# Layer 3's first counts, first batch and last batch rearranged in a four-layer graph kernel

## What is computed

```
x = ln(x + L0(x, adj))   # 8 Euler steps of a graph diffusion
x = ln(x + L1(x, adj))   # two-layer graph network with batch norm
x = ln(x + L2(x, adj))   # attention, 4 heads, masked by adj
x = ln(x + L3(x, adj))   # graph attention:
    Wh = x @ W;  s1 = Wh @ a1;  s2 = Wh @ a2
    e  = leaky_relu(s1[i] + s2[j], 0.2), masked by adj
    h  = softmax(e) @ Wh
```

## Time and profile before

| | us |
|---|---|
| median of 3 executions | 977.42 (976.46 to 977.71) |
| the profiled execution, its own time | 978.22 |
| its span from the first to the last instruction | 976.2 |
| TensorE busy | 902.6 (92%) |
| VectorE busy | 638.6 (65%) |
| ScalarE busy | 508.6 (52%) |
| GpSimd busy | 387.3 (40%) |
| TensorE's granted clock, mean | 0.964 of 2.4 GHz |

### The profile page before, as it was taken

How to read it: one execution, slowest core, us unless ns; L and a number is a source line. 1 busy time by engine, 2 the same in 40 slices (tenths; PEclk the granted TensorE clock), 3 DMA queues, 4 the chain that set the end, 5 groups by cost and what they waited for, 6 DMA issues and landing times. The chain is left out here.

```text
span 976.2 us, 20907 instructions
## 1 busy us (share of the span) xinstructions
PE 902.6 (92%) x6004; PEld 647.9 (66%) x6020; DVE 638.6 (65%) x1936; ACT 508.6 (52%) x918; POOL 387.3 (40%) x439
## 2 busy tenths in 40 slices
PE   6999999999999699975789999999999989999994
PEld 5799999999999688732345445554455533677774
DVE  4754554554554676655557777777777753899995
ACT  4323121121121345664356777777777755888883
POOL 4011121021020130000246777777787855365556
PEclk9999999999999899988579999999999998999998
DMA  8000000000000100000033343333433331010111
GB/s 242 22 12 12 12 22 12 16 16 11 22 0 0 39 5 0 0 1 1 19 80 66 74 91 65 81 81 67 95 65 81 82 69 31 12 29 25 32 32 43
DMA packets 34219, 40.66 MB, mean 42 GB/s; under 512 B 6656, under 2 KB 17536, under 8 KB 34176
## 3 DMA queue, kind: packets, MB, share of 16 engines
q1 hardware_dynamic: 33072, 40.00, 17.2%
q10 hardware_dynamic: 1104, 0.13, 0.1%
HBM read 6.43 MB, written 4.19 MB: 11 GB/s over the span
## 5 line engine op out<-in xcount | busy, mean ns | idle before, releaser
L1681 DVE CUSTOM_DVE_ANT_0 junk<-bank,mask_ij 128x512 bf16<-128x512 f32 x256 | 166.6, 688 | 78.9 <-PE bank L1763 76.9
L1546 POOL TENSOR_TENSOR half_sum<-prob 128x1024 f32<-128x1024 f32 x64 | 151.7, 2379 | 15.6 <-ACT prob L1619 13.6
L1619 ACT ACTIVATE prob<-wide 128x1024 f32<-128x1024 f32 x128 | 125.2, 1017 | 39.4 <-PE wide L1780 35.9
L431 ACT CAST yT<-wide 128x512 fp32r<-128x512 f32 x48 | 28.1, 589 | 206.1 <-PE wide L827 156.7
L531 POOL TENSOR_TENSOR Xr<-Xf,Xr 128x512 fp32r<-128x512 f32 x16 | 20.4, 1291 | 168.1 <-ACT Xr L426 167.9
L1763 PE MATMUL bank<-qkT 32*128 32x512 f32 x256 | 79.6, 516 | 7.9 <-DVE mx L1681 6.9
L1776 PE MATMUL wide<-qk_st 128*128 128x512 f32 x256 | 76.9, 423 | 1.0 <-issue 0.7
L1373 PEld LDWEIGHTS bank<-Wh,pr 128*128 128x128 f32 x512 | 65.3, 191 | 14.6 <-ACT pr L1260 6.8
L1373 PE MATMUL bank<-Wh,pr 128*128 128x129 f32 x512 | 68.5, 278 | 5.6 <-ACT pr L1260 4.8
L59 PE MATMUL bank<-z,L3T_hi 128*128 128x256 f32 x256 | 73.3, 286 | 0.3 <-DVE zf L646 0.3
L153 POOL TENSOR_SCALAR n_rstd<-n_aggr 128x4 f32<-128x4 f32 x32 | 6.7, 209 | 167.5 <-DVE n_aggr L146 162.0
(11 more groups left out here) (289 smaller groups left out, 2265.2 us busy)
## 6 DMA issues: line engine op xcount, KB each, us to landing
qk_st<-qkT SPq DMA_DIRECT2D x192, 128.0 KB, 2.4
out_dram<-rc SPq DMA_DIRECT2D x16, 256.0 KB, 2.3
Xf<-X SPq DMA_DIRECT2D x14, 256.0 KB, 2.3
A<-in_adj_dram SPq DMA_DIRECT2D x4, 256.0 KB, 5.0
qk_st<-neg_row SPq DMA_DIRECT2D x64, 2.0 KB
Xf<-in_x_dram SPq DMA_DIRECT2D x2, 256.0 KB, 6.8
mask_q<-mask_ji SPq DMA_DIRECT2D x16, 32.0 KB, 1.8
w<-in_L_gnn_W_dram SPq DMA_DIRECT2D x2, 128.0 KB, 2.2
```

The lines of the kernel that those rows point to most:

```text
L1546: pool.tensor_tensor(flat(half_sum[h][:]), flat(prob[bp][h][:, 0:2]), flat(prob[bp][h][:, 2:4]), ALU.add).then_inc(h_sum, 1)
L1619: act.activation(flat(prob[bp][h][:, 2 * half:2 * half + 2]), wide[half][:], ACT.Exp, scale=SCALE).then_inc(t_exp, 1)
L1681: dve.tensor_tensor_reduce(out=junk[hh][:], in0=bank[4 + hh][:], in1=m.mask_ij[:, i], scale=1.0, scalar=3.0 * MASKED, op0=ALU.add, op1=ALU ...
```

## The change

Six things are done.

1. The three calls that give layer 3's semaphores their first counts move to the head of each engine's program in the block, ahead of layer 2's items and layer 2's own first counts.
2. For batch 0, both halves of Wh lie in banks 4 and 5 (`half`) and the s1 rows in bank 4 (`s1_bank`), in place of banks 0 and 1. So `w1.0` waits for the row maxima of batch 0 (bank 5 held the s2 rows) and no longer for the seventh exponential of batch 15; `i.0` waits for `W0.0`; `q0.0` waits for the four relus of batch 0 and `q1.0` for both copies of Wh. `x.1` and `i.1` now wait for the eighth exponential.
3. The last batch's second pair of exponentials is done tile by tile, and its `a` items wait for each.
4. The last batch's residuals, statistics and aggregations are done in two halves (`dve_last`), and GpSimd only takes the roots (`pool_last_root`), by halves.
5. The scaling of batches 14 and 15 is done on VectorE in place of GpSimd.
6. The last batch is stored in two halves, the first by SyncE and the second by ScalarE.

The hand-written lists and the orders of the loops are not changed.

```diff
+    last_eps, last_rstd, last_x, last_stored = (sem(f"last_{x}") for x in ("eps", "rstd", "applied", "stored"))
+    LAST = B - 1
...
     def half(b, k):
-        return bank[0] if k else bank[4] if is_batch(b, 0) else bank[3]
+        return bank[4 + k] if is_batch(b, 0) else bank[0] if k else bank[3]
+
+    def s1_bank(b):
+        return bank[4] if is_batch(b, 0) else bank[1]
...
-        pairs(sp, B, 1, step)
+        pairs(sp, LAST - 1, 1, step)
+        step(LAST - 1, 0, [True], LAST // 2)
+        sp.wait_ge(last_x, 2)
+        sp.dma_start(half_of_out(0), r[1][:, 0:2]).then_inc(stored[1], 16)
+        sp.wait_ge(last_stored, 16)
...
+    def act_last_store(act):
+        act.wait_ge(last_x, 4)
+        act.dma_start(half_of_out(1), r[1][:, 2:4]).then_inc(last_stored, 16)
...
+    def pool_last_root(pool):
+        rstd, aggr = norm.rstd[1], norm.aggr[1]
+        pool.wait_ge(norm.s_x, after(LAST - 2, 4))
+        for h in range(2):
+            two = slice(2 * h, 2 * h + 2)
+            pool.wait_ge(norm.s_aggr, after(LAST, 4, 2 * h + 2))
+            hold(pool, gate)
+            pool.tensor_scalar(rstd[:, two], aggr[:, two, 1], EPS, 1.0, ALU.add, ALU.mult).then_inc(last_eps, 1)
+            pool.wait_ge(last_eps, h + 1)
+            pool.tensor_tensor(rstd[:, two], rstd[:, two], m.neg_half[:, 0:2], ALU.pow).then_inc(last_rstd, 1)
...
+    def act_last(act, item):
+        item("L3", LAST, 1, LAST // 2)
+        item("E0", LAST, 1, LAST // 2)
+        for k in range(2, NT):
+            act.wait_ge(e_s, after(LAST, NT, k + 1))
+            act.activation(pr[1][:, k], pr[1][:, k], ACT.Exp).then_inc(ex, 1)
+        act_last_store(act)
...
+    def dve_last(dve, item):
+        for h in range(2):
+            for name in (f"d{h}", f"r{2 * h}", f"r{2 * h + 1}"):
+                item(name, LAST, 1, LAST // 2)
+            dve.wait_ge(res, after(LAST, NT, 2 * h + 2))
+            for k in range(2 * h, 2 * h + 2):
+                dve.bn_stats(norm.stats[1][:, k], r[1][:, k]).then_inc(norm.s_stats, 1)
...
+            for k in range(2 * h, 2 * h + 2):
+                dve.bn_aggr(norm.aggr[1][:, k], norm.stats[1][:, k]).then_inc(norm.s_aggr, 1)
+        norm.apply(dve, LAST - 1 + CREDIT, 0, r[0], lambda k: r[0][:, k])
+        for h in range(2):
+            dve.wait_ge(last_rstd, h + 1)
+            hold(dve, gate)
+            for k in range(2 * h, 2 * h + 2):
+                dve.tensor_scalar(r[1][:, k], r[1][:, k], norm.aggr[1][:, k, 0:1], norm.rstd[1][:, k:k + 1],
+                                  ALU.subtract, ALU.mult).then_inc(last_x, 1)
...
             if what == "x":
+                if is_batch(b, 1):
+                    pe.wait_ge(*ready["second wide"])
...
             elif what == "w":
                 if is_batch(b, 0) and k == 1:
-                    pe.wait_ge(*ready["first wide"])
+                    pe.wait_ge(s_mx, after(0, NT))
...
             elif what == "i":
                 if is_batch(b, 0):
-                    pe.wait_ge(*ready["first wide"])
-                pe.matmul(bank[1][:], wB[0][:], xT[par][:], start=True, stop=True).then_inc(s1_ps, 1)
+                    pe.wait_ge(wh_c, after(0, 2, 1))
+                if is_batch(b, 1):
+                    pe.wait_ge(*ready["second wide"])
+                pe.matmul(s1_bank(b)[:], wB[0][:], xT[par][:], start=True, stop=True).then_inc(s1_ps, 1)
...
             elif what == "q":
+                if is_batch(b, 0) and k == 0:
+                    pe.wait_ge(relu, after(0, NT))
+                if is_batch(b, 0) and k == 1:
+                    pe.wait_ge(wh_c, after(0, 2))
...
         @block.tensor
         def _(pe):
+            third.pe_credits(pe)
             for s in (b_ps, x_ps, q_ps, k_ps, v_ps, n_ps[0], n_ps[1], o_ps, d_ps):
                 pe.sem_inc(s, CREDIT)
...
             run(pe, PE_ORDER, work, last=17)
-            third.pe_credits(pe)
```

More of the change, by code:

```diff
@@ L1182, in step, with half_of_out @@
                              r[par][:]).then_inc(stored[par], 16)
-        pairs(sp, B, 1, step)
+        pairs(sp, LAST - 1, 1, step)
[3 more added lines that the diff above has]
+        sp.wait_ge(last_stored, 16)
         for k in range(2):
             sp.wait_ge(stored[k], 16 + 16 * (B // 2))
+    def half_of_out(h):
+        return out[LAST:LAST + 1].rearrange("a (t p) d -> p (a t) d", p=P)[:, 2 * h:2 * h + 2]
+    def act_last_store(act):
+        act.wait_ge(last_x, 4)
+        act.dma_start(half_of_out(1), r[1][:, 2:4]).then_inc(last_stored, 16)
     def pool_constants(pool):
@@ L1202, in pool_copy @@
         pool.tensor_copy(flat(Xf[par][:]), batch_flat(m.X, s)).then_inc(x_f, 1)
+    def pool_last_root(pool):
[8 more added lines that the diff above has]
+            pool.tensor_tensor(rstd[:, two], rstd[:, two], m.neg_half[:, 0:2], ALU.pow).then_inc(last_rstd, 1)
     def pool_norm(pool, b, par, copied):
         pool.wait_ge(x_f, after(copied, 1))
+        if isinstance(b, int) and b == LAST:
+            pool_last_root(pool)
+            return
         norm.root(pool, b + CREDIT, par)
+        if isinstance(b, int) and b == LAST - 1:
+            return
         norm.apply(pool, b + CREDIT, par, r[par], lambda k: r[par][:, k])
@@ L1248, in item @@
                     act.wait_ge(e_s, after(b - 2, NT))
-                act.activation(rl[par][:, k], bank[1][:], ACT.Relu, scale=1.0 - SLOPE,
+                act.activation(rl[par][:, k], s1_bank(b)[:], ACT.Relu, scale=1.0 - SLOPE,
                                bias=Wh[par][:, k, S2_REST:S2_REST + 1]).then_inc(relu, 1)
@@ L1321, in dve_items @@
         return item
+    def dve_last(dve, item):
[5 more added lines that the diff above has]
+                dve.bn_stats(norm.stats[1][:, k], r[1][:, k]).then_inc(norm.s_stats, 1)
+            dve.wait_ge(norm.s_stats, after(LAST, 4, 2 * h + 2))
+            hold(dve, gate)
[4 more added lines that the diff above has]
+            dve.wait_ge(last_rstd, h + 1)
+            hold(dve, gate)
+            for k in range(2 * h, 2 * h + 2):
+                dve.tensor_scalar(r[1][:, k], r[1][:, k], norm.aggr[1][:, k, 0:1], norm.rstd[1][:, k:k + 1],
+                                  ALU.subtract, ALU.mult).then_inc(last_x, 1)
     def pe_credits(pe):
@@ L1362, in item @@
                 if is_batch(b, 0):
-                    pe.wait_ge(*ready["first wide"])
-                pe.matmul(bank[1][:], wB[0][:], xT[par][:], start=True, stop=True).then_inc(s1_ps, 1)
+                    pe.wait_ge(wh_c, after(0, 2, 1))
+                if is_batch(b, 1):
+                    pe.wait_ge(*ready["second wide"])
+                pe.matmul(s1_bank(b)[:], wB[0][:], xT[par][:], start=True, stop=True).then_inc(s1_ps, 1)
             elif what == "a":
                 h, t = divmod(k, 2)
-                pe.wait_ge(ex, after(b, 2))
+                one_by_one = isinstance(b, int) and b == LAST
+                pe.wait_ge(ex, after(b, 2, 1 if one_by_one else 2))
                 pe.wait_ge(res, after(b - 1, NT, 2 * h + 2))
@@ L1372, in item @@
                 for j in range(NT):
+                    if one_by_one and j >= 2:
+                        pe.wait_ge(ex, after(LAST, 2, j))
                     last = pe.matmul(out_bank[h][:, t * (D + 2):t * (D + 2) + D + 1],
@@ L1387, in layer3 @@
     third.act_items, third.dve_items, third.pe_items = act_items, dve_items, pe_items
+    third.act_last, third.dve_last = act_last, dve_last
     third.in_order, third.const = in_order, const
@@ L1449, in layers2_3 @@
                        {"O": (bn, after(B - 1, 1)), "X": norm.s_x, "score banks": (s_mx, after(B - 1, TILES)),
-                        "first wide": (t_exp, after(B - 1, EXPS, EXPS - 1)), "second wide": (t_exp, after(B - 1, EXPS)),
+                        "second wide": (t_exp, after(B - 1, EXPS)),
                         "ring": ((rcp, after(B - 1, 1)), (o_n, after(B - 1, 1)))})
@@ L1567, in _ @@
         def _(act):
+            third.act_credits(act)
             for s in (bn, x_hi, x_c, q_hi, k_hi, v_c, n_row[0], n_row[1], o_c, d_c):
@@ L1636, in _ @@
             run(act, ACT_ORDER, work, last=17)
-            third.act_credits(act)
             item = third.act_items(act)
@@ L1640, in _ @@
                  "3L1.0 3X.1 e.15 3L2.0 y.14 3L3.0 f.15 3E0.0 3W0.1 3W1.1 3E1.0 3XR.2 3G.1 3L0.1 3L1.1 3X.2 3L2.1 y.15", ACT_ORDER, work, item)
-            pairs(act, B, 4, third.in_order(item, third.act_order), first=3)
+            pairs(act, B, 4, third.in_order(item, third.act_order), last=B, first=3)
+            third.act_last(act, item)
         @block.vector
         def _(dve):
+            third.dve_credits(dve)
             for s in (res1, q_lo, k_lo, rcp, o_n):
@@ L1706, in _ @@
                  "3c1.1 b.15", DVE_ORDER, work, item)
-            pairs(dve, B, 3, third.in_order(item, third.dve_order), first=2)
+            pairs(dve, B, 3, third.in_order(item, third.dve_order), last=B, first=2)
+            third.dve_last(dve, item)
         @block.tensor
```

(1 more changed line is left out.)

1 line of the change is left out of this document (removed).

## The result

The change made the kernel slower: 979.9 us in the median of 20 executions (978.23 to 982.35) against 977.68 of 20 (976.46 to 978.82), a ratio of 1.0024 (95% interval 1.0018 to 1.003). The forecast was 974.1, faster, in a range of 971.8 to 976.6. The profiled execution took 979.92 us, its span is 978.1 against 976.2.

What follows compares the result with a forecast made beforehand. Busy TensorE kept the loops near their limit; the seam's `x_ps` chain and a serial last batch cost time. +0.4 - 7.1 + 4.5 + 1.7 - 2.8 = -3.3, so 974.1 us against 977.42, range 971.8 to 976.6.

Steps and rivals of the forecast that it cites:

- The credits at their old place: Seam of layers 2 and 3: with `x_ps` counted early, `D0.14` starts sooner at full clock; `t1.15` 7.1 us earlier.
- Rival 4: Seam: another count holds GpSimd's copy, so the 7.1 us gain is lost; 979.5 to 981.2 us, chance 0.05.
- Batch 0 in the score banks: Seam: `w1.0` waits for the row maxima and `q0.0` for the four relus; +4.5 us.
- The clock in this stall: TensorE's stall before `q0.0`: the granted clock falls, costing between nothing and 2.9 us; taken as +1.7 us.
- Rival 2: Seam: clock falls early, before `w1.0`, with `D0.15`/`D1.15` at half rate; 2 to 3 us over forecast, 976.6, chance 0.13.
- The credits at their new place: Head of layer 2: six more TensorE increments before ScalarE's first item is released; 0 to 0.65 us, taken as +0.4.
- Exponentials in smaller steps: Last batch: finer exponentials gain nothing, since VectorE's first residual waits for the store of batch 13; 0.
- The end: Last batch: halves and VectorE scaling end the last scaling at 970.2 instead of 973.15; taken as -2.8 us.
- Rival 3: End: VectorE's scalings and GpSimd's powers stand in a line at their shared port; 975.1 us, chance 0.08.

Runs made afterwards that it cites:

- e4: The changed kernel with useless TensorE matmuls, 11 ahead of `w1.0`'s wait and 12 ahead of `q0.0`'s, the waits kept: 974.66 us, ratio 0.9968.
- e5: The changed kernel with batch 0's old banks and, of layer 3's first counts, only `x_ps` given early, behind TensorE's own of layer 2: 968.07 us.
- e9: e5 with the last batch's second pair of exponentials in one instruction again: 968.08 us, ratio 0.9899.
- e10: e5 with batch 15's residual in a slot of its own, so it waits for no store of batch 13: 967.19 us, ratio 0.9897.
- e11: e10 with the last batch's second pair of exponentials in one instruction: 968.58 us, ratio 0.9906.
- e8: The kernel before with the new end alone (exponentials by tile, two halves, VectorE scaling, two stores): 974.26 us, ratio 0.9969.

## Why the prediction was wrong

*The credits at their old place*, -7.1: right, -7.2, in every kernel with `x_ps` early (12.64 to 12.70 us from memset to `t1.15`). Rival 4 is out. The measured time lies in its band of 979.5 to 981.2, but that is chance: the 7 us that it says are lost were gained.

*Batch 0 in the score banks*, +4.5 for the two waits: right, 4.3 with the clock held (e4). Stalls of 2.5 and 2.65 us were foreseen and 2.55 and 2.3 came.

*The clock in this stall*, +1.7, bounded by 2.9: **this is the step that failed.** It measured 5.3. The forecast put one fall, into the second stall, and took the clock in the first stall as held, a term of nothing. The second fall cost 1.6, as priced. The first, priced at nothing, cost 3.7: about 2 us in `w1.0` to `j.1` (from the start of `w1.0` to `D0.15` it is 5.2 us, and 3.1 in e4) and 1.7 us in `D0.15` and `D1.15`, which stand ahead of `e.15` and so of the relus that `q0.0` waits for. Rival 2 had this mechanism at a chance of 0.13, but counted only the 1.9 us of `D0.15` and `D1.15`, and so stopped at 976.6. A row for it was on the table: the stretch from 492 to 496, with idleness of this size, had brought a fall, and I used it for one stall and not for the other. The Trainium skill (TensorE: Matmul & The Clock Gate, the section on HAM oscillation) tells of a loop in which every wait for a transfer between bursts of matmuls, of 3 to 5 us there, puts TensorE back to its low clock. The trace agrees in kind, at shorter waits: two stalls of 2.55 and 2.3 us, two falls.

*The credits at their new place*, +0.4: too small. Two things were added up as one: `N.0` 0.4 us later, as foreseen, and `T.0` another 0.5, which fits TensorE being still at its own increments when `N.0` was done (one increment in e5 makes 0.16 us of it, six make 0.47). That is 0.9. The remaining 1.6 us arose inside layer 2's fill, together with a lower mean clock there (0.70 against 0.82). Why the clock stays low longer is open: no run shifted the fill by itself or held its clock, and the level changes between executions of the same instructions too. That early credits favour the low levels is likely from the fourteen profiles, and not shown.

*Exponentials in smaller steps*, 0: right (e5 against e9), for the reason given (e10 against e11).

*The end*, -2.8: by itself 3.6 (e8), of which 0.3 lie behind the last scaling, where I had kept everything as it was. In the changed kernel's profile 2.4, because the store of batch 13 landed 1.1 us late there; it landed in 2.3 us in e5 to e8, and in 2.8 in e4. Why it landed late is open. Rival 3, scalings and powers in a line, did not come: GpSimd's power at 973.84 and VectorE's scalings at 973.31 and 974.34 overlap, at 0.77 and 1.11 us, against 0.69 for the power before it, at 972.31, and 1.12 for the same four in the earlier trace rows. The Trainium skill (SBUF — State Buffer, the section on who interferes with whom), which I had weighed there, has `tensor_scalar` contend with GpSimd in its two-port modes. This form showed no block; whether it ran in such a mode no run shows.

With the measured terms the sum is 0.9 + 1.6 - 7.2 + 4.3 + 5.3 - 2.4 = +2.5, against a difference of 2.2 between the medians and 2.0 between the spans, where the block began 0.5 earlier.

## What to carry to other kernels

A bank given to a later user also gives that user's predecessor a new wait, and the price is set by what stands ahead of the releasing instruction in its engine's queue: here two copies and a layer norm ahead of two relus. Price every TensorE stall together with the clock for the items behind it, and let no stall go at a price of nothing because a longer one follows: here each brought its own fall, and the dearer fall was the one ahead of work that the next wait hung on. And first counts in front of a pipeline's first item delay that item (0.9 us for all of them here), so move only the one that somebody waits for.

## What the runs showed that I had not expected

Twenty-three useless matmuls in two waits made the kernel 5.2 us faster (979.9 to 974.66). And layer 2's fill without its head, the same instructions with the same waits, took from 333.7 to 337.1 us by profile, more than most edits here are worth, in step with a mean clock from 0.82 down to 0.63 between 492 and 520. It differs even between kernels whose programs are the same up to there, so a difference of 1 us between two single profiles of this kernel says little.
